# Backward direction stored time-reversed, so that one scan instruction serves both directions of a pair

## The reference

```python
x, z = split(seq @ in_w.T)                 # 128 inner channels
x = silu(causal_conv(x) + conv_b)          # 4 taps along the sequence
dt, B, C = split(x @ xp_w.T)               # 4, 16, 16 columns
delta = softplus(dt @ dt_w.T + dt_b)
for t in range(128):                       # 128 channels x 16 states
    h = exp(delta[t] * A) * h + (delta[t] * x[t]) * B[t]
    y[t] = sum_over_states(h * C[t])
out = ((y + x * D) * silu(z)) @ out_w.T
```

## Time and profile before

| | us |
|---|---|
| median of three runs | 27994.34 |
| span of the profiled execution, first to last instruction | 27985.0 |
| its excess over the span, median of the runs less span | 9.3 |
| VectorE busy | 25924.2 (93%) |
| GpSimd busy | 25531.3 (91%) |
| TensorE busy | 18123.9 (65%) |
| ScalarE busy | 16971.9 (61%) |
| mean granted clock of TensorE | 0.80 of full speed |

### The profile page before, as it was taken

The page is one execution under the profiler, slowest core; times in us unless marked ns, Lnnn a source line. Parts: engine busy times, 40 slices in busy tenths (PEclk is TensorE's granted clock), DMA queues, the critical chain, the costliest instruction groups (busy, mean ns, idle before and its releaser), DMA issues. The chain is left out here.

```text
span 27985.0 us, 284715 instructions
## 1 busy us (share of the span) xinstructions
PE 18123.9 (65%) x62778; PEld 5245.1 (19%) x62778; DVE 25924.2 (93%) x24107; ACT 16971.9 (61%) x23653; POOL 25531.3 (91%) x11268
## 2 busy tenths in 40 slices
PE   6666666666666666666666666666666666666572
PEld 1111111111111111111111111111111111111120
DVE  8999999999999999999999999999999999999321
ACT  6666666666666666666666666666666666665232
POOL 8999999999999999999999999999999999999000
PEclk8888888888888888888888888888888888887786
DMA  5555555555555555555555555555555555555967
GB/s 188 200 199 200 199 199 199 197 198 199 199 200 199 200 197 200 199 197 197 198 199 199 200 199 199 198 200 197 196 199 199 200 199 199 198 199 182 186 131 179
DMA packets 1915003, 5473.38 MB, mean 196 GB/s; under 512 B 214002, under 2 KB 642818, under 8 KB 1901458
## 3 DMA queue, kind: packets, MB, share of 16 engines
q1 hardware_dynamic: 1912968, 5451.83, 57.5%
HBM read 4644.92 MB, written 805.60 MB: 195 GB/s over the span
## 5 line engine op out<-in xcount | busy, mean ns | idle before, releaser
L793 POOL TENSOR_TENSOR drive<-du_rep,b_rep 128x1024 f32<-128x1024 f32 x8192 | 19125.7, 2363 | 314.6 <-DVE state L726 186.1
L726 DVE TENSOR_TENSOR_SCAN decay<-decay,drive 128x512 f32<-128x512 f32 x10752 | 12618.1, 1211 | 127.9 <-POOL drive L793 65.0
L596 ACT ACTIVATE decay<-delta_rep,a_neg 128x1016 f32<-128x1016 f32 x8192 | 8994.7, 1106 | 594.0 <-DMA delta_rep<-delta_spread 465.9
L450 PE MATMUL y_bank<-read,sel_f 128*32 128x512 f32 x32768 | 5366.0, 786 | 2009.7 <-DVE gated L748 1800.0
L739 DVE TENSOR_TENSOR read<-decay,c_rep 128x1024 f32<-128x1024 f32 (+1 forms) x5632 | 6490.4, 1152 | 0.0
L726 DVE TENSOR_TENSOR_SCAN state<-decay,drive 128x512 f32<-128x512 f32 x5120 | 6164.5, 1204 | 0.4 <-ACT decay L596 0.2
L806 POOL TENSOR_TENSOR read<-state,c_rep 128x1024 f32<-128x1024 f32 x2560 | 6040.9, 2360 | 0.1
L592 ACT COPY decay<-zeros 128x8 f32<-128x8 f32 x5632 | 946.2, 168 | 6944.2 <-DVE read L739 6897.3
L427 PE MATMUL p_bank<-e_one,sel_f 128*128 128x512 f32 x2048 | 1607.6, 877 | 2801.9 <-ACT e_one L577 2610.8
L414 PE MATMUL p_bank<-u,to_dt 128*128 128x512 f32 x2048 | 1527.4, 836 | 1898.7 <-ACT vpos L540 1252.7
L404 PE MATMUL p_bank<-xt,taps 128*128 128x512 f32 x4096 | 2082.3, 630 | 1002.1 <-ACT u L535 521.0
(11 more groups left out here) (109 smaller groups left out, 14258.1 us busy)
## 6 DMA issues: line engine op xcount, KB each, us to landing
du_rep<-du_spread SPq DMA_DIRECT2D x2048, 512.0 KB, 6.2
delta_rep<-delta_spread SPq DMA_DIRECT2D x2048, 512.0 KB, 5.5
b_rep<-bc_spread SPq DMA_DIRECT2D x2048, 512.0 KB, 7.6
c_rep<-bc_spread SPq DMA_DIRECT2D x2048, 512.0 KB, 4.3
du_spread<-e_log SPq DMA_DIRECT2D x512, 512.0 KB, 2.7
delta_spread<-e_one SPq DMA_DIRECT2D x512, 512.0 KB, 3.6
xt<-in_xs SPq DMA_DIRECT2D x1024, 128.0 KB, 3.5
bc_spread<-bc SPq DMA_DIRECT2D x1024, 64.0 KB, 1.6
```

The source lines that it names most:

```text
L450: mm = nc.tensor.matmul(y_bank[32 * j:32 * j + 32, :], gather, read[:, (ROW * m + j) % READ_RING, px(d)], start=(m == 0 and d == FWD), sto ...
L596: nc.scalar.activation(inner(place[:, :]), inner(delta_rep[:, j, :]), ACT.Exp, scale=a_neg[s][:, ROW * j + m:ROW * j + m + 1]).then_inc(s_ ...
L726: nc.vector.tensor_tensor_scan(to[:, ::step], decay[PLACE[h][q]][:, px(d)][:, ::step], drive[:, q % DRIVE_RING, px(d)][:, ::step], 0.0, AL ...
L793: nc.gpsimd.tensor_tensor(drive[:, q % DRIVE_RING, :], du_rep[h][:, j, :], b_rep[:, m, :], ALU.mult).then_inc(s_drive, 1)
```

## The change

The backward half is kept in the order of time instead of the order of pixels: TensorE writes it reversed within each sequence when it convolves (`conv` reads the input with step -1), and turns it back when it sums into `y_bank` (`in_order` in `add_ud` and `sum_row`). What lies in between runs forward. One scan of 1024 columns then serves both directions of a pair, and the semaphore of states counts pairs instead of halves. The first column of each sequence is at a multiple of 128 in both halves (`inner`, `firsts`).

VectorE's order in a pair is then: scan of q, read of q-1. Pair 15 is read whole by VectorE, after scan 0 of the next unit (`read_last`); GpSimd reads its five pairs and no half. The decay places are numbered without a break through all tiles (`place_of`, with the tile's number modulo 3 as `turn`), so that each place was last used by the pair three before.

```diff
+def place_of(turn, h, q):
+
+    return (2 * PAIRS * turn + PAIRS * h + q) % DECAY_RING
+
+
+def place_before(q):
+
+    n = q - DECAY_RING
+    return n % PAIRS, int(n < 0)
...
-            return bass.AP(ap.tensor, ap.offset,
-                           [list(ap.ap[0]), [WIDE - HALF + SIDE - 1, 2], [SIDE, USEQS]])
+            return bass.AP(ap.tensor, ap.offset, [list(ap.ap[0]), [SIDE, 2 * USEQS]])
+
+        def in_order(ap, d):
+
+            return ap if d == FWD else ap.rearrange("p (s t) -> p s t", t=SIDE)[:, :, ::-1]
...
-                offs = (3, 1) if d == FWD else (4, 6)
+                offs, step = ((3, 1), 1) if d == FWD else ((4, 6), -1)
                 for m in range(2):
                     mm = nc.tensor.matmul(p_bank[:, :], taps[s][:, 2 * d + m, :],
-                                          xt[:, :, offs[m]:offs[m] + SIDE],
+                                          xt[:, :, offs[m]:offs[m] + SIDE][:, :, ::step],
...
-                    mm = nc.tensor.matmul(y_bank[:, :], d_diag[s][:, :], u[h][:, px(d)],
+                    mm = nc.tensor.matmul(y_bank[:, :], d_diag[s][:, :], in_order(u[h][:, px(d)], d),
...
-                                              read[:, (ROW * m + j) % READ_RING, px(d)],
+                                              in_order(read[:, (ROW * m + j) % READ_RING, px(d)], d),
...
-            def make_decay(U, h, s, q):
+            def make_decay(U, h, s, q, turn):
                 m, j = group_of(q)
-                place = decay[PLACE[h][q]]
-                _, n, back = place_before(h, q)
+                place = decay[place_of(turn, h, q)]
+                n, back = place_before(q)
                 if n in BY_POOL:
 
-                    at_least(act, s_state, 2 * PAIRS * (U - back) + 2 * n + 2)
+                    at_least(act, s_state, PAIRS * (U - back) + n + 1)
                 else:
-                    if n == SHARED:
-                        at_least(act, s_state, 2 * PAIRS * (U - back) + 2 * n + 2)
 
                     at_least(act, s_read_v, NV * (U - back) + vector_before(n) + 1)
...
-            def scan(U, h, q, d):
-                if d == FWD:
-                    dve.wait_ge(s_decay, PAIRS * U + q + 1)
-                    dve.wait_ge(s_drive, PAIRS * U + q + 1)
+            def scan(U, h, q, turn):
+                dve.wait_ge(s_decay, PAIRS * U + q + 1)
+                dve.wait_ge(s_drive, PAIRS * U + q + 1)
                 n = pool_before(q)
                 if q in BY_POOL:
 
                     last = n - STATE_RING
-                    at_least(dve, s_read_g, (NG + 1) * (U + last // NG) + last % NG + 1)
+                    at_least(dve, s_read_g, NG * (U + last // NG) + last % NG + 1)
                     out = state[:, (NG * h + n) % STATE_RING, :]
                 else:
-                    out = decay[PLACE[h][q]][:, :]
-                step = 1 if d == FWD else -1
-                to = out[:, px(d)]
-                if q == SHARED and d == REV:
-
-                    at_least(dve, s_read_g, (NG + 1) * U)
-                    to = state_half[:, :]
-                nc.vector.tensor_tensor_scan(to[:, ::step],
-                                             decay[PLACE[h][q]][:, px(d)][:, ::step],
-                                             drive[:, q % DRIVE_RING, px(d)][:, ::step], 0.0,
+                    out = decay[place_of(turn, h, q)][:, :]
+                nc.vector.tensor_tensor_scan(out, decay[place_of(turn, h, q)][:, :], drive[:, q % DRIVE_RING, :], 0.0,
                                              ALU.mult, ALU.add).then_inc(s_state, 1)
 
-            def read_state(U, h, q):
+            def read_state(U, h, q, turn):
 
                 m, j = group_of(q)
                 dve.wait_ge(s_c[m], 16 * (U + 1))
 
                 at_least(dve, s_ysum, ROW * U + m - 1)
-                part = px(FWD) if q == SHARED else slice(0, WIDE)
-                dve.wait_ge(s_state, 2 * PAIRS * U + 2 * q + (1 if q == SHARED else 2))
-                nc.vector.tensor_tensor(read[:, q % READ_RING, part], decay[PLACE[h][q]][:, part],
-                                        c_rep[:, m, part], ALU.mult).then_inc(s_read_v, 1)
+                dve.wait_ge(s_state, PAIRS * U + q + 1)
+                nc.vector.tensor_tensor(read[:, q % READ_RING, :], decay[place_of(turn, h, q)][:, :],
+                                        c_rep[:, m, :], ALU.mult).then_inc(s_read_v, 1)
+
+            def read_last(U, h, turn):
+                if PAIRS - 1 not in BY_POOL:
+                    read_state(U, h, PAIRS - 1, turn)
...
-                        scan(U, h, q, FWD)
+                        scan(U, h, q, turn)
+                        if q == 0 and not (prev is None and h == 0):
+                            read_last(U - 1, 1 - h, turn - 1 + h)
                         if q > 0 and q - 1 not in BY_POOL:
-                            read_state(U, h, q - 1)
-                        scan(U, h, q, REV)
-                        if q == PAIRS - 1:
-                            read_state(U, h, q)
+                            read_state(U, h, q - 1, turn)
                         if q == GATE and not (prev is None and h == 0):
...
-                if q == SHARED:
-                    nc.gpsimd.tensor_tensor(read[:, q % READ_RING, px(REV)], state_half[:, :],
-                                            c_rep[:, m, px(REV)], ALU.mult).then_inc(s_read_g, 1)
-                    return
```

More of the change, by code:

```diff
@@ L62, in group_of @@
     return divmod(q, ROW)
-SHARED = PAIRS - 1
 def vector_before(q):
     return sum(1 for n in range(q) if n not in BY_POOL)
[L73 to L80, removed]
+def place_of(turn, h, q):
[3 more added lines that the diff above has]
+    return n % PAIRS, int(n < 0)
 def pool_before(q):
@@ L87, in reads_by_pool @@
 def reads_by_pool(q):
-    return pool_before(q) + (q > SHARED)
+    return pool_before(q)
 class Step:
@@ L110 @@
 DECAY_RING = 3
-PLACE = [[(PAIRS * h + q) % DECAY_RING for q in range(PAIRS)] for h in range(2)]
 GATHER = (4, 8, 12)
@@ L209, in scan_stage @@
         s_drive = sem("drive_ready")
-        s_state = sem("state_halves")
+        s_state = sem("states_scanned")
         s_read_v = sem("read_by_vector")
@@ L223, in inner, with turn @@
             return bass.AP(ap.tensor, ap.offset + 1,
-                           [list(ap.ap[0]), [HALF - 1, 2], [SIDE, USEQS], [1, SIDE - 1]])
+                           [list(ap.ap[0]), [SIDE, 2 * USEQS], [1, SIDE - 1]])
         def firsts(ap):
-            return bass.AP(ap.tensor, ap.offset,
-                           [list(ap.ap[0]), [WIDE - HALF + SIDE - 1, 2], [SIDE, USEQS]])
+            return bass.AP(ap.tensor, ap.offset, [list(ap.ap[0]), [SIDE, 2 * USEQS]])
+        def in_order(ap, d):
+            return ap if d == FWD else ap.rearrange("p (s t) -> p s t", t=SIDE)[:, :, ::-1]
         block = ctx.enter_context(nc.Block())
         def over_tiles(engine, body, tail):
-            body(0, None, 0, 0)
+            def turn(i):
+                return i % DECAY_RING
+            body(0, None, 0, 0, turn(0))
             with engine.Fori(0, (TILES - 2) // ROUND) as k:
                 for n in range(ROUND):
-                    body(ROUND * k + 1 + n, 0, 0, 0)
-            body(TILES - 1, 0, 0, 1)
-            body(TILES, 0, 1, 1)
+                    body(ROUND * k + 1 + n, 0, 0, 0, turn(1 + n))
+            body(TILES - 1, 0, 0, 1, turn(TILES - 1))
+            body(TILES, 0, 1, 1, turn(TILES))
             with engine.Fori(0, (TILES - 2) // ROUND) as k:
                 for n in range(ROUND):
-                    body(ROUND * k + TILES + 1 + n, 1, 1, 1)
-            body(2 * TILES - 1, 1, 1, None)
+                    body(ROUND * k + TILES + 1 + n, 1, 1, 1, turn(TILES + 1 + n))
+            body(2 * TILES - 1, 1, 1, None, turn(2 * TILES - 1))
             tail(2 * TILES)
@@ L340, in _, with body @@
                 load_c(0, m)
-            def body(i, prev, cur, nxt):
+            def body(i, prev, cur, nxt, turn):
                 for U, h, w_prev, w_next, w_next2 in units(i, prev, cur, nxt):
@@ L443, in sum_row @@
                 pe.wait_ge(s_read_v, NV * U + vector_before(ROW * m + ROW))
-                pe.wait_ge(s_read_g, (NG + 1) * U + reads_by_pool(ROW * m + ROW))
+                pe.wait_ge(s_read_g, NG * U + reads_by_pool(ROW * m + ROW))
                 if m == 0:
@@ L627, in _ @@
             for q in range(AHEAD):
-                make_decay(0, 0, 0, q)
+                make_decay(0, 0, 0, q, 0)
             def take(s, use, before, U, h, w_prev, w_next, w_next2):
@@ L660, in body @@
                         if ahead < PAIRS:
-                            make_decay(U, h, cur, ahead)
+                            make_decay(U, h, cur, ahead, turn)
                         elif w_next is not None:
-                            make_decay(U + 1, 1 - h, w_next, ahead - PAIRS)
+                            make_decay(U + 1, 1 - h, w_next, ahead - PAIRS, turn + h)
```

(13 more changed lines are left out.)

4 lines of the change are left out of this document (1 added, 3 removed).

## The result

The changed kernel takes 28513.96 us (median of 4, 28502.16 to 28515.83) against 27992.15 for the kernel before on the same chip: ratio 1.0185, 95% interval 1.0171 to 1.0200. It is slower by 1.85%, as forecast; the forecast was 28465.

A forecast was written before the change was run, and what follows sets the result against it. VectorE (93% busy) and GpSimd (91%) nearly full, VectorE waiting for others. Per unit (half tile, 16 pairs): 49.16 work plus waits 1.23, 0.74, 0.12 = 51.25 us, +0.92; times 512, +471 us: 28465 us, range 28080 to 28770.

The forecast's parts named there:

- present waits: VectorE's waits before the change, 0.91 us per unit, put down to the broken ring of decay places.
- The long scan: On VectorE, one 1024-column scan takes 2.194 us between starts, against 2 x 1.122; saves 0.80 us per unit.
- the rival: Long scan on VectorE saves a duration's whole constant part, taking 2.117 us: 27994 us, no change; chance 0.05.
- (a) decay 12: Before scan 12, VectorE arrives after 5.42 us, ScalarE's chain from read 8 takes 6.65: wait 1.23 us per unit.
- (b): Unit's first du product on VectorE waits 0.74 us for ScalarE's two decays and copy after read 0.
- (c): Unit's second du product on VectorE waits 0.12 us: 2.69 us after read 3, against ScalarE's 2.81.
- level: First du's other path, read 14 through TensorE's eight matmuls and copy: 8.7 us against 8.73 on VectorE; 0.03 added.
- Unbroken ring: Numbering decay places without a break removes VectorE's 0.91 us of waits per unit, leaving 49.16 us.
- spare time: GpSimd, freed of its half read, needs 1.2 us less per unit; as it won't be the bound, nothing more gained.
- Reversed reads on TensorE cost nothing: TensorE's matmuls on reversed columns take no longer; the rival, double cost, 29390 us, had chance 0.04.
- The sum: Per unit, 49.16 + 1.23 + 0.74 + 0.12 = 51.25 us, +0.92 on 50.33.
- in place of none: GpSimd's share falls to about 87%, with waits for VectorE's states where it was said to have none before.

The follow-up runs named there:

- e1: Changed kernel with Exp in place of both SiLUs of the step z, so no table loads in the loop: 27925.11 us, ratio 0.9978.
- e4: Changed kernel with each scan as two halves again and the read of the pair before between them: 27822.57 us, ratio 0.9942.
- e5: Changed kernel with read 8 moved directly behind scan 8, ahead of scan 9: 28143.22 us, ratio 1.0056.
- e9: Changed kernel with the scan of pair 9 alone in two halves, read 8 between them: 28152.32 us, ratio 1.0063.
- e2: Kernel before the change, with Exp in place of both SiLUs of the step z: 27956.44 us, ratio 0.9990.
- e7: Changed kernel with reads 0, 3, 8 and 14 each one scan earlier: 27789.06 us, ratio 0.9932.
- e6: Changed kernel with reads 0 and 3 each one scan earlier: 28420.50 us, ratio 1.0158.
- e10: Changed kernel with the scans of pairs 1, 4, 9 and 15 in two halves, reads 0, 3, 8 and 14 between them: 27638.33 us, ratio 0.9878.
- e3: Kernel before the change, with the unbroken ring of decay places alone: 27769.20 us, ratio 0.9923.
- e11: Changed kernel with the first du product one pair later on VectorE: 28423.82 us, ratio 1.0160.

## Why the prediction was right

The time is 49 us off (28514 against 28465), and the steps hold one by one but for the present waits, where one premise was wrong:

- *The long scan*: 2.194 forecast, 2.19 measured. The duration did shrink by 0.127, to 2.287 = 2 x 1.207 - 0.127, just as with two sizes of read. The interval shrank by 0.05 alone, from 2 x 1.122 = 2.244, and the rival needed 0.127 of the interval.
- *(a) decay 12*: 1.23 forecast, 1.24 in the unit shown, 1.26 in the mean. e1 takes it away on ScalarE, e4, e5 and e9 on VectorE, and e2 shows that the loads cost next to nothing where VectorE comes later. e5 and e9 gave back only 60% of it, because the chain's next starting point, the convolution, was close behind: where VectorE still waits in the units looked at of e5, e7 and e9, ScalarE goes from the convolution's u to decay 12 without a gap. That VectorE waited 0.05 us there before, 6.65 against 6.60, was read from a group's 3.48 us; its third scan lasts 1.23 instead of 1.20, so the wait was 0.02 to 0.03. The forecast does not rest on it.
- *(b) and (c), the du products*: 0.74 and 0.12 forecast, 0.72 and 0.12 measured in the mean. That (b) is ScalarE's chain is right for this kernel by the rows of its copy; no run shows it alone, since in e6 TensorE's sum took its place. That TensorE's was "level" was right only for a burst as fast as in the earlier trace rows: in e6 it is 0.7 us behind VectorE and not 0. e7 and e10, which also start it sooner, remove the wait.
- *Unbroken ring*: the forecast took all 0.91 us of present waits for the ring's and said that they go. e3 shows it for the wait at du (0.66 us per unit, 0.03 left). The 0.18 us at scan 0 belong to the turn of the loop, and the ring left them in place. In the changed kernel they went all the same: 26 us are left before scans 0 and 2 of the 93. There GpSimd has time to spare, while in the kernel before and in e3 it had next to none; that this is the reason was not tested. The forecast called this spare time worth nothing, so in this term of 0.18 us the number is right by luck.
- *Reversed reads on TensorE cost nothing*: in the changed kernel the four matmuls of the forward convolution take 2.00 us in the median and the four on reversed columns 1.98; e7's rows at the full clock show the same pair. The sums of reads, half of them reversed, went from a mean of 786 to 770 ns. Before and after:

```profile
L450 PE MATMUL y_bank<-read,sel_f 128*32 128x512 f32 x32768 | 5366.0, 786 | 2009.7 <-DVE gated L748 1800.0 <-POOL read L806 169.4 <-POOL read L803 15.2
L452 PE MATMUL y_bank<-read,sel_f 128*32 128x512 f32 x32768 | 5243.0, 770 | 1852.8 <-DVE gated L742 1817.0 <-DVE read L729 25.1 <-POOL read L796 10.6
```

- *The sum*: 51.25 forecast, 51.36 measured. Of the missing 0.11 us, 0.05 is VectorE's own work (49.21 against 49.16: its tiles of 512 columns take 0.60 and not 0.58), 0.05 the waits at the turns of the loop, and 0.03 the longer mean at scan 12; the first du takes 0.02 back.

I expected GpSimd to wait for states "in place of none". Before, it was idle for 315 us before drives, 186 of them for states, and now for 1390: it has 2.8 us per unit to spare.

## What to carry to other kernels

Merging two instructions saved the constant part of an interval (0.05 us here, not the 0.13 of a duration), and it moves what stood between them. Before merging, take each buffer that the middle instruction frees. Compare the time until its next user wants it with the length of the chain that must refill it: an engine that is busy 61% of the time can hold one of 93% at a single place. Where few places are tight, merge everywhere else and keep the split there: twelve long scans and four split ones beat sixteen of either kind. Read a wait over many units before naming its cause: the one at scan 0 was put down to the ring, but it came once in twelve units, at the turn of the loop.

## What the runs showed that was not expected

A read that stands directly behind the scan whose result it reads starts 0.20 us late (e5). TensorE's eight-matmul burst takes 3.7 us straight behind other work. In the rows shown it takes 5.8 to 6.7 after 3.5 to 4.6 us of idling, and over the units of the changed kernel 5.1 to 6.8. So moving a consumer later can make its producer slower (e11). And e6 and e11, which differ in what they move, ended within 4 us of each other (28420.5 and 28423.8). The waits differ in kind but add up to the same: 0.73 + 1.23 us per unit in e6, 0.68 + 1.29 in e11. Why the sums agree is open.
